# Decoder layer on one core: head halves outside and batches inside, 512-column projections, the last stages of a batch beside the next batch's attention

## The chip, the core and the metric

The kernel runs on one core of a Trainium2 chip. The metric is the device time of one execution in microseconds (us). TensorE (PE) does the matmuls, VectorE (DVE), ScalarE (ACT) and GpSimd (POOL) the rest, and SyncE (SP) issues the transfers. Each engine works through its own list of instructions in order and waits on semaphores for the others.

## The reference

One decoder layer with post-norm on x of 4 batches, 256 tokens and 256 channels, in fp32:

```python
x = _layernorm(x + attn(x))      # 16 heads of 128; q, k with rmsnorm; causal mask and ALiBi bias
x = _layernorm(x + xattn(x, ctx))
x = _layernorm(x + ffn(x))
# attn
q, k = rmsnorm(x @ Wq, q_rms_w), rmsnorm(x @ Wk, k_rms_w)
scores = q @ k.T / sqrt(128) - slope[h] * dist      # causal
y = rmsnorm(softmax(scores) @ (x @ Wv), subln_w)
attn = y @ Wproj                 # 2048 to 256
# xattn: attention = softmax((ctx Wq' + bq)(ctx Wk' + bk)'), result[l, m] = sum_n x[l, n] attention[m, n]
# ffn: 256 to 1024 to 256; weights quantised to -1, 0, 1 times their mean size, inputs to 8 bits by row
h = sigmoid(bitlinear(x, w_gate)) * bitlinear(x, w_up); out = bitlinear(h, w_down)
```

## The kernel before

**Preparation.** The contexts' queries, keys, energies and exponentials are made first, and x is turned into `xT_hi` and `xT_lo`, two parts whose products with `w_hi` and `w_lo` (three for each of two blocks of 128 channels: six matmuls) give the projection.

**Attention.** There are 64 steps. Head by head (outside), batch by batch (inside), a step n projects q, k and v of one head and batch, 384 columns for each of two token tiles (`qkv(0)` and `qkv(1)`, L482), and carries three earlier ones on: of n-1 the normed q and k are turned (L493) and the scores made (L505, L506), of n-2 the probabilities are turned (L499) and multiplied with v (L512 to L514), of n-3 the normed y is turned (L521). VectorE adds a bias with the mask and finds the negative maximum in one operation (L835), norms q and k (L791) and y (L812), copies the turned probabilities (`pT`, L817) and sums squares (L797, L804). ACT takes squares (L635, L673), exponentials and copies. GpSimd raises sums to -1/2 (`qk_rstd` L315, `y_rstd` L310), splits the next head's weights into high and low parts (L276, L280) and halves the bias in place. The steps run in a hardware loop of eight, seven trips, after eight steps written out. The weights of a head are loaded once; three feed-forward pieces are rounded, turned and copied in each trip. Every turned y is kept in `yT` (64 of them).

**Tail.** The output projection (L422, 16 heads for each of eight token tiles, two passes for each fp32 matmul) is done afterwards: four tiles' worth starts while the last heads drain, the others fill TensorE between the last stages. These run tile by tile, `m` in 0 to 8, each half a tile behind the other: residual and layer norm (moments L845, L846; GpSimd's power L355; application on VectorE L851), `x1T`, mixing with the cross attention (L557), norm, quantising (L900 to L904), gate and up (L587), hidden product (L865), its maximum (L886), rounding on ACT (L694), `hq` (L895), `hT` (L564), down (L572, L908), norm and store.

The order of every engine's work is written out by hand; there is no planner.

Of the kernel before, what the change touches and what calls it, by code (L numbers as in the profile page):

```python
# [14 lines left out]
P = 128  # L35
# [3 lines left out]
BANK = 512  # L39


def decoder_kernel(nc, x, ctx_in, wq, wk, wv, wproj, q_rms, k_rms, subln, xwq, xbq, xwk, xbk,
# [10 lines left out]
    STEPS = H * B  # L53
    PAIR = 2 * B
    TRIPS = H // 2
    EARLY = -(-TT * H // 6)
    CROSS_STEP = 3
    FF_STEP = 5
    SPLITS = 3
    VW = D + 1  # L60
    S0, S1 = slice(0, P), slice(P, 3 * P)
    SLOPE0 = 2.0 ** -0.5
    assert D == P and CC == P and T == 2 * P and C == 2 * P and B == 4 and H % 2 == 0
    assert TRIPS == FC and FF_STEP + 3 == PAIR

    ctx = ExitStack()
    with ctx:
# [3 lines left out]
        def sem(name):  # L71
            return ctx.enter_context(nc.semaphore(name))


# [3 lines left out]
        w_raw = sb("w_raw", [P, 2, KC, 3, D])  # L78
        w_hi = sb("w_hi", [P, 2, KC * 3 * D], F32R)
        w_lo = sb("w_lo", [P, 2, KC * 3 * D], F32R)  # L80
        bias = sb("bias", [P, 2, 3 * P])
        wp = sb("wp", [P, H, C])
        yT = sb("yT", [P, STEPS, T])
# [3 lines left out]
        minus_half = sb("minus_half", [P, TT])  # L87
        vecs = sb("vecs", [P, 7])
        bq_col, bk_col, qk_scale, sub_scale = vecs[:, 3:4], vecs[:, 4:5], vecs[:, 5:6], vecs[:, 6:7]
        sq = sb("sq", [P, TT, 2, D + 1])  # L90
        sqy = sb("sqy", [P, TT, VW])
        qk_sum, qk_rstd = sb("qk_sum", [P, TT, 2]), sb("qk_rstd", [P, TT, 2])
        y_sum, y_rstd = sb("y_sum", [P, TT]), sb("y_rstd", [P, TT])
        qk_n = sb("qk_n", [P, TT, 2, D])
        qT = sb("qT", [P, T])
        kT = sb("kT", [P, T])
# [4 lines left out]
        v_sb = sb("v_sb", [P, B, TT, VW])  # L101
        y_n = sb("y_n", [P, TT, D])


        prep = yT[:].rearrange("p n t -> p (n t)")
        ctx_sb = prep[:, 0:NT * CC].rearrange("p (n c) -> p n c", n=NT)
        ctxT = prep[:, 1024:1024 + B * T]
        qcT = prep[:, 2048:2048 + B * T]
        kcT = prep[:, 3072:3072 + B * T]
        xw_sb = prep[:, 4096:4096 + 2 * CC].rearrange("p (a c) -> p a c", a=2)  # L110
        xwT = prep[:, 4352:4352 + 2 * CC].rearrange("p (a c) -> p a c", a=2)
        attn_sum = prep[:, 4608:4608 + NT]
        abs_w = prep[:, 5120:5120 + F]
        attn_raw = prep[:, 11264:11264 + NT * T].rearrange("p (n t) -> p n t", n=NT)
        attn = sb("attn", [P, NT, T])
        neg_xmax = sb("neg_xmax", [P, NT])
# [4 lines left out]
        ff_round = sb("ff_round", [P, C])  # L121
        ff_q = sb("ff_q", [P, C], BF16)
        w_sum = sb("w_sum", [P, 6])
        w_total = sb("w_total", [P, 3])
        w_scale = sb("w_scale", [P, 3])
        w_inv = sb("w_inv", [P, 3])


        res = sb("res", [P, 3, C])
        stats = sb("stats", [P, 3, nc.vector.BN_STATS_DIM])  # L130
        mean_var = sb("mean_var", [P, 3, 2])
        var_eps = sb("var_eps", [P, 3])
        ln_rstd = sb("ln_rstd", [P, 3])
        x1 = sb("x1", [P, C])
        x2 = sb("x2", [P, 2, C])
        fin = sb("fin", [P, 2, C])
        x1T = sb("x1T", [P, KC, P])
        x_most, x_scale, x_inv, h_most, h_scale, h_inv, down_scale = (sb(n, [P, 1]) for n in (
            "x_most", "x_scale", "x_inv", "h_most", "h_scale", "h_inv", "down_scale"))
        gate_up_scale = sb("gate_up_scale", [P, 2])  # L140
        round_col, table = sb("round_col", [P, 1]), sb("table", [P, 1])
        x_round = sb("x_round", [P, C])
        xq = sb("xq", [P, C], BF16)
        xqT = sb("xqT", [P, KC, P], BF16)

        sig, hid, h_round = ff_raw[:, 0, 0:F], ff_raw[:, 0, F:2 * F], ff_raw[:, 1, 0:F]
        hq = sb("hq", [P, F], BF16)
        hT = sb("hT", [P, FC, P], BF16)
# [784 lines left out]
```

## Time and profile before

| what | us |
|---|---|
| median of three runs | 435.4 (434.58 to 435.41) |
| profiled execution, span from the first to the last instruction | 432.9 |
| TensorE busy | 401.9 (93%) |
| VectorE busy | 327.7 (76%) |
| ACT busy | 254.4 (59%) |
| GpSimd busy | 220.2 (51%) |

The page gives each engine's busy time and the chain of work that ended last, followed back from the last instruction. The windows give the same busy times for a stretch, with the clock that TensorE was granted there (1.00 is full) and what the transfers moved. The chain in order of time gives each instruction only the time by which the next link was later, so for TensorE it is issue time, while a matmul's duration in the timeline also has its way through the array and overlaps with the next.

### The profile page before, as it was taken

What the parts mean: (1) busy time and instruction counts of PE and PEld (TensorE: products, weight loads), DVE (VectorE), ACT (ScalarE), POOL (GpSimd) and SP (SyncE); (2) the same over time, 40 slices, a digit from 0 to 9 for tenths busy, and PEclk for the clock granted to TensorE, in tenths of its full rate; (3) what the DMA queues carried; (4) which work ended last, traced back from release to release, by engine and by line L of the source; (5) the groups of instructions that cost most, each with busy time, mean ns of one, the idle gap of its engine ahead of it and who ended that gap; (6) DMA issues with size and microseconds to landing.
All of it is one profiled execution on the core that took longest, in us unless ns stands there. A gap on an engine that the chain in (4) does not pass through costs nothing.

```text
span 432.9 us, 9595 instructions
## 1 busy us (share of the span) xinstructions
PE 401.9 (93%) x2605; PEld 361.1 (83%) x2612; DVE 327.7 (76%) x1000; ACT 254.4 (59%) x750; POOL 220.2 (51%) x368
## 2 busy tenths in 40 slices
PE   4979999999999999999999999999999899999552
PEld 3668899999999999999999999999988677777321
DVE  0777987887797798788779779878822788888862
ACT  3486777677676776767767677676722333333321
POOL 3633667676675776767767677675501122222210
PEclk9999999999999999999999999999999999999965
DMA  8980010110101101011010110000000000000000
GB/s 223 316 251 2 2 36 3 38 37 0 36 0 36 36 0 36 0 36 36 0 36 0 36 36 0 0 0 0 0 2 0 2 0 15 12 14 12 13 14 24
DMA packets 21747, 14.52 MB, mean 34 GB/s; under 512 B 1760, under 2 KB 21472, under 8 KB 21728
## 3 DMA queue, kind: packets, MB, share of 16 engines
q1 hardware_dynamic: 21728, 14.29, 11.2%
q8 instruction: 9, 0.15, 0.2%
q14 instruction: 10, 0.08, 0.1%
HBM read 13.24 MB, written 1.05 MB: 33 GB/s over the span
## 4 chain that ended last, share of the span: by engine, by line
PE 86%; DVE 5%; ACT 4%; issue 2%; DMA 1%; POOL 1%; SPq 0%; POOLq 0%; DVEq 0%
PE ps L482 30%; PE ps L422 11%; PE ps L493 7%; PE ps L506 6%; PE ps L499 5%; PE ps L512 4%; PE ps L505 3%; PE ps L514 3%; PE ps L513 3%; PE ps L521 3%; PE ps L587 3%; PE ps L572 2%; ACT hT L696 2%; DMA x_sb<-in_x 1%; PE ps L557 1%
## 5 line engine op out<-in xcount | busy, mean ns | idle before, releaser
L315 POOL TENSOR_TENSOR qk_rstd<-qk_sum,minus_half 128x2 f32<-128x2 f32 x128 | 88.5, 692 | 92.6 <-DVE qk_sum L797 90.8
L482 PE MATMUL ps<-w_hi,xT_hi 128*128 128x384 f32 x256 | 96.9, 378 | 2.3 <-DVE qk_n L791 1.4
L482 PE MATMUL ps<-w_hi,xT_lo 128*128 128x384 f32 x256 | 86.5, 338 | 0.0
L482 PE MATMUL ps<-w_lo,xT_hi 128*128 128x384 f32 x256 | 86.3, 337 | 0.0
L797 DVE TENSOR_REDUCE qk_sum<-sq 128x2 f32<-128x258 f32 x128 | 53.6, 419 | 30.8 <-ACT sq L635 29.1
L635 ACT ACTIVATE sq<-ps 128x256 f32<-128x256 f32 x128 | 49.1, 384 | 34.6 <-PE ps L482 34.4
L791 DVE TENSOR_TENSOR qk_n<-ps,qk_rstd 128x256 f32<-128x256 f32 x128 | 54.2, 423 | 18.8 <-POOL qk_rstd L315 17.8
L422 PE MATMUL ps<-wp,yT 128*128 128x256 f32 x256 | 62.2, 382 | 0.0
L310 POOL TENSOR_TENSOR y_rstd<-y_sum,minus_half 128x2 f32<-128x2 f32 x64 | 49.0, 766 | 24.6 <-DVE y_sum L804 20.9
L673 ACT ACTIVATE sqy<-ps 128x258 f32<-128x258 f32 x64 | 24.8, 387 | 58.5 <-PE ps L514 58.5
L422 PEld LDWEIGHTS ps<-wp,yT 128*128 128x128 f32 x256 | 46.7, 190 | 5.9
L482 PEld LDWEIGHTS ps<-w_hi,xT_hi 128*128 128x128 f32 x256 | 48.4, 189 | 3.0 <-DVE qk_n L791 1.7
L482 PEld LDWEIGHTS ps<-w_lo,xT_hi 128*128 128x128 f32 x256 | 48.6, 190 | 0.0
L482 PEld LDWEIGHTS ps<-w_hi,xT_lo 128*128 128x128 f32 x256 | 48.0, 188 | 0.0
L352 POOL TENSOR_SCALAR var_eps<-mean_var 128x1 f32<-128x1 f32 x24 | 7.0, 292 | 79.6 <-DVE mean_var L846 79.6
L835 DVE CUSTOM_DVE_ANT_0 score<-ps,bias 128x128 f32<-128x128 f32 (+1 forms) x128 | 40.3, 352 | 2.8 <-PE ps L506 2.8
L493 PE MATMUL ps<-ident,qk_n 128*128 128x128 f32 x256 | 38.7, 273 | 0.8 <-DVE qk_n L791 0.6
L506 PE MATMUL ps<-kT,qT 128*128 128x256 f32 x128 | 38.2, 380 | 0.0
L280 POOL TENSOR_TENSOR w_lo<-w_raw,w_hi 128x256 fp32r<-128x256 f32 x48 | 35.4, 738 | 4.0
L817 DVE COPY pT<-ps 128x384 f32<-128x384 f32 x64 | 35.1, 548 | 2.6 <-PE ps L499 2.5
L493 PEld LDWEIGHTS ps<-ident,qk_n 128*128 128x128 f32 x256 | 31.1, 140 | 5.0 <-issue 3.2
L639 ACT COPY v_sb<-ps 128x128 f32<-128x128 f32 x128 | 34.0, 266 | 0.0
(126 smaller groups left out, 846.9 us busy)
## 6 DMA issues: line engine op xcount, KB each, us to landing
w_raw<-in_L_attn_Wq SPq DMA_DIRECT2D x16, 128.0 KB, 2.2
w_raw<-in_L_attn_Wk SPq DMA_DIRECT2D x16, 128.0 KB, 2.3
w_raw<-in_L_attn_Wv SPq DMA_DIRECT2D x16, 128.0 KB, 2.3
wp<-in_L_attn_Wproj SPq DMA_DIRECT2D x1, 2048.0 KB, 16.1
ff_raw<-in_L_ffn_w_gate SPq DMA_DIRECT2D x1, 1024.0 KB, 8.6
ff_raw<-in_L_ffn_w_up SPq DMA_DIRECT2D x1, 1024.0 KB, 11.0
ff_raw<-in_L_ffn_w_down SPq DMA_DIRECT2D x1, 1024.0 KB, 13.0
out<-fin SPq DMA_DIRECT2D x8, 128.0 KB, 1.7
```

The source lines that it names most:

```text
L280: pool.tensor_tensor(lo, raw, hi, ALU.subtract).then_inc(s_split, 1)
L310: pool.tensor_tensor(y_rstd[:], y_sum[:], minus_half[:], ALU.pow).then_inc(s_ry, 1)
L315: pool.tensor_tensor(qk_rstd[:, t, :], qk_sum[:, t, :], minus_half[:], ALU.pow).then_inc(s_rs[t], 1)
L422: last = pe.matmul(ps[:, u % 2, 0:C], yT[:, h * B + b, t * P:(t + 1) * P], wp[:, h, :], start=(h == 0), stop=(h == H - 1))
L482: last = pe.matmul(ps[:, t, 0:3 * D], xa[:, k, tok], wa[:, r, k * 3 * D:(k + 1) * 3 * D], start=(i == 0), stop=(i == len(parts) - 1))
L493: last = pe.transpose(dst[:, t * P:(t + 1) * P], qk_n[:, t, a, :], ident[:])
L506: pe.matmul(ps_s[:, S1], qT[:, P:T], kT[:], start=True, stop=True).then_inc(s_s, 1)
L635: act.activation(sq[:, t, :, 0:D], ps[:, t, 0:2 * D].rearrange("p (a d) -> p a d", a=2), ACT.Square).then_inc(s_sq[t], 1)
L791: dve.tensor_tensor(qk_n[:, t], ps[:, t, 0:2 * D].rearrange("p (a d) -> p a d", a=2), r, ALU.mult).then_inc(s_qkn[t], 1)
L797: dve.tensor_reduce(qk_sum[:, t, :], sq[:, t], AX.X, ALU.add).then_inc(s_ss[t], 1)
L817: dve.tensor_copy(pT[:], ps_pT).then_inc(s_pT, 1)
L835: last = dve.tensor_tensor_reduce(score[:, s], ps_s[:, s], bias[:, r, s], 1.0, 3e38, ALU.add, ALU.min, neg_max[:, t:t + 1])
```

## The change

Outside are now two halves of the heads, inside the four batches, and innermost the eight heads of a half: eight blocks of eight steps, all written out without a loop. The six pieces of weights of a half (four of two heads' q and k, two of four heads' v) are split once and stay resident, 512 columns each. The query-key projection of a step (three steps ahead, `LAG`) makes one token tile of two heads; every second step has a value projection of four heads and one tile. ACT and VectorE split the first half's pieces with GpSimd; in steps 24 to 30 VectorE makes the high part and GpSimd the low part of the second half's.

The output projection of a step follows three steps later into one bank, summed over the eight heads of a block; the first half's sum is added onto `x_sb` in place. `wp` is multiplied by `sub_scale` beforehand. After the second half's block of a batch its two tiles go through the last stages in steps of their own offsets from `late_start` (the second tile four steps after the first, for the last batch both together), beside the next batch's attention. Layer norms are applied on GpSimd, and so is `x_round`. Sigmoid becomes tanh of half the argument, with the factors folded into scales. The cross attention's preparation moves from the start into slots "a", "b" and "c" of steps 3 to 16, the feed-forward weights' into steps 12 to 24, 1024 columns at a time by two comparisons instead of eight trips of 256.

Banks: A and B take the projections, TB the turned q, k and also the turned y, SP the scores and also the turned probabilities, Y the values' product, O the output projection, F and G the side work. For the last batch's two tiles SP, Y, TB, O and A, B, F, G are used.

The order in a step n, by engine. TensorE: `project_qk(n + 3)`; q and k of n turned; the probabilities of n-1 turned; `project_v` in even steps; slot "a"; output projection of n-3; y of n-2 turned; slot "b"; scores of n; values' product of n-1; slot "c". VectorE: `norm(n + 2)`; `y_sum` of n-2; the first half's `split_low`; late work of the tiles at offset 1 (residual, moments), 2 (`xq`), 3 (hidden half 0), 4 (hidden half 1, maximum, scales), 6 (residual, moments); `y_n` of n-2; `pT` of n-1; `qk_sum` of n+3; `split_high`; slot "a"; `wp` scaled (steps 1 and 30); `sum_ff`; `quantise_ff`; slot "b"; the block's sum added (and, in the second half, moments); score operations of n; `x_most` (offset 1), `hq` (offset 4). ACT: square of y; exponentials of n-1; cross exponentials (steps 9 to 12); tanh half 0; squares of n+3; `split_high` of the first half; `qT`, `kT`; value copy; slot "a"; `h_round` (offset 4); `yT`; slot "b"; tanh half 1.

```diff
+LAG = 3
+PREP = {
+    -4: (("a", "x", 0),), -3: (("a", "x", 1),), 0: (("a", "x", 2),), 1: (("a", "x", 3),),
+    3: (("a", "xw", 0),), 4: (("a", "ctx", 0), ("b", "ctx", 1)),
+    5: (("a", "qc", 0), ("b", "qc", 1)), 6: (("a", "kc", 0), ("b", "kc", 1)),
+    8: (("a", "en", 0),), 9: (("a", "en", 1),), 10: (("a", "en", 2),), 11: (("a", "en", 3),),
+    13: (("a", "at", 0),), 14: (("a", "at", 1),), 15: (("a", "at", 2),), 16: (("a", "at", 3),),
+    17: (("a", "ws", 0),),
+    19: (("a", "ff", 0),), 20: (("a", "ff", 1),), 21: (("a", "ff", 2),), 22: (("a", "ff", 3),),
+    23: (("a", "ff", 4),), 24: (("a", "ff", 5),),
+}
+FIRST_SPLIT = {-4: (0, 1), -3: (2,), -1: (3,), 0: (4,), 1: (5,)}
+SECOND_SPLIT = {24: 6, 25: 7, 26: 8, 28: 9, 29: 10, 30: 11}
+LATE_STEPS = 7
+LATE_SLOTS = ((0, "a", "x1T"), (0, "c", "mix"), (2, "a", "xqT"), (2, "c", "gate0"), (2, "c", "up0"),
+              (3, "b", "gate1"), (3, "b", "up1"), (5, "a", "hT"), (5, "c", "down"))
...
+    def late_start(tile):
+        b, t = tile // TT, tile % TT
+        start = HB * (B + b) + HB + LAG
+        return start if b == B - 1 else start + 4 * t
...
+            sp.dma_start(x_sb[:, 0:TT, :], x_d[:, 0:TT, :]).then_inc(s_x[0], 16)
+            for c in range(3):
+                load_piece(c)
+            sp.dma_start(x_sb[:, TT:NT, :], x_d[:, TT:NT, :]).then_inc(s_x[1], 16)
+            load_wp(0)
+            for c in range(3, 6):
+                load_piece(c)
...
+            for n in steps():
+                if 0 <= n - 2 < N:
+                    pool.wait_ge(s_ssy, n - 1)
+                    wait(pool, s_yn, n - 2)
+                    pool.tensor_tensor(y_rstd[:], y_sum[:], minus_half[:, 0:TT], ALU.pow).then_inc(s_ry, 1)
+                for c in FIRST_SPLIT.get(n, ()):
+                    split_first(c)
+                if n in SECOND_SPLIT:
+                    split_second(SECOND_SPLIT[n], (0, 1))
+                for tile in late(n, 1):
+                    wait(pool, s_mv[2], tile - 2)
+                    layer_norm(1, tile, res2, x2[:, tile % 3])
...
+                    pool.tensor_tensor(qk_rstd[:, t], qk_sum[:, t], minus_half[:], ALU.pow).then_inc(s_rs, 1)
+                if n in SECOND_SPLIT:
+                    split_second(SECOND_SPLIT[n], (2, 3))
...
+                    pe.wait_ge(s_qkT, n + 1)
+                    wait(pe, s_pT, n)
+                    pe.matmul(ps_s[:, S0], qT[:, 0:P], kT[:, 0:P], start=True, stop=True)
+                    pe.matmul(ps_s[:, S1], qT[:, P:T], kT[:], start=True, stop=True).then_inc(s_s, 1)
...
+                for tile in late(n, 4):
+                    t = tile % TT
+                    hidden(tile, 1)
...
+                    link(dve.tensor_reduce(h_most[:, t:t + 1], hid[:, t], AX.X, ALU.max, apply_absolute_value=True))
...
+                    dve.tensor_tensor(y_n[:], ps_y[:, :, 0:D], y_rstd[:].unsqueeze(2).to_broadcast([P, TT, D]),
                                       ALU.mult).then_inc(s_yn, 1)
...
+                    dve.tensor_copy(pT[:], ps_s).then_inc(s_pT, 1)
...
+                if n in SECOND_SPLIT:
+                    split_high(SECOND_SPLIT[n])
...
+                if 18 <= n < 24:
+                    quantise_ff(n - 18)
```

## Rows read from the trace of the kernel before

**Rows 1.** Windows: us of each engine, TensorE's granted clock, transfers' share and GB/s.

```profile
10.00:20.00 10.00, 10.00 (x39) 6.85 (x39) 6.51 (x14) 4.86 (x13) 6.67 (x12) 1.00 1.02 302
100.00:200.00 100.00, 100.00 (x707) 96.27 (x706) 82.31 (x270) 69.73 (x229) 68.73 (x107) 1.00 0.07 20
400.00:420.00 20.00, 12.44 (x65) 6.88 (x64) 14.81 (x40) 7.15 (x11) 4.54 (x10) 0.83 0.04 14
420.00:433.00 13.00, 2.92 (x16) 1.80 (x16) 4.42 (x11) 2.25 (x2) 0.74 (x2) 0.56 0.06 20
```

**Rows 2.** Chain in order of time, 214 to 217 us: start, issue time, what.

```profile
214.48 0.44 PE ps L493 x4
214.92 0.33 PE ps L499 x3
215.25 1.06 PE ps L482 x6
216.31 0.22 PE ps L505 x2
216.53 0.43 PE ps L506 x2
```

**Rows 3.** Timeline of one attention step, TensorE and VectorE: start, duration.

```profile
208.76 0.42 PE L482 MATMUL ps<-w_hi,xT_hi 128*128 128x384 f32 x1
...
211.00 0.42 DVE L812 TENSOR_TENSOR y_n<-ps,y_rstd 128x256 f32<-128x256 f32 x1
...
211.35 0.55 DVE L817 COPY pT<-ps 128x384 f32<-128x384 f32 x1
...
212.73 0.28 DVE L835 CUSTOM_DVE_ANT_0 score<-ps,bias 128x128 f32<-128x128 f32 x1
...
212.94 0.42 DVE L835 CUSTOM_DVE_ANT_0 score<-ps,bias 128x256 f32<-128x256 f32 x1
...
213.18 0.42 PE L482 MATMUL ps<-w_hi,xT_hi 128*128 128x384 f32 x1
```

**Rows 4.** Timeline of TensorE in the tail, 361 to 365 us.

```profile
361.51 1.03 PE L587 MATMUL ps<-wuT,xqT 128*128 128x512 bf16 x4
362.38 1.89 PE L422 MATMUL ps<-wp,yT 128*128 128x256 f32 x8
364.10 0.38 PE L550 MATMUL ps<-ident,x 128*128 128x128 f32 x2
```

**Rows 5.** Groups by line and shape: busy us, mean ns; idle time before.

```profile
L315 POOL TENSOR_TENSOR qk_rstd<-qk_sum,minus_half 128x2 f32<-128x2 f32 x128 | 88.5, 692 | 92.6 <-DVE qk_sum L797 90.8
...
L280 POOL TENSOR_TENSOR w_lo<-w_raw,w_hi 128x256 fp32r<-128x256 f32 x48 | 35.4, 738 | 4.0
...
L865 DVE SCALAR_TENSOR_TENSOR ff_raw<-ps,gate_up_scale,ff_raw 128x512 f32<-128x512 f32 x16 | 11.9, 747 | 3.2 <-PE ps L587 2.9
...
L895 DVE TENSOR_SCALAR hq<-ff_raw 128x1024 bf16<-128x1024 f32 x8 | 5.5, 683 | 1.4 <-ACT ff_raw L694 1.4
...
L720 DVE TENSOR_TENSOR xT_lo<-ps,xT_hi 128x512 fp32r<-128x512 f32 x4 | 2.7, 689 | 12.3 <-ACT xT_hi L596 12.3
```

**Rows 6.** Timeline of VectorE after the last attention step.

```profile
326.67 0.42 DVE L804 TENSOR_REDUCE y_sum<-sqy 128x2 f32<-128x258 f32 x1 [3.12 <-ACT sqy L673]
327.89 0.42 DVE L812 TENSOR_TENSOR y_n<-ps,y_rstd 128x256 f32<-128x256 f32 x1 [0.80 <-POOL y_rstd L310]
```

**Rows 7.** Timeline of VectorE for the last tile.

```profile
404.91 0.39 DVE L876 TENSOR_TENSOR res<-ps,x_sb 128x256 f32<-128x256 f32 x1
...
408.18 1.22 DVE L886 TENSOR_REDUCE h_most<-ff_raw 128x1 f32<-128x1024 f32 x1
...
409.82 0.41 DVE L891 TENSOR_TENSOR res<-ps,x 128x256 f32<-128x256 f32 x1
...
410.73 0.18 DVE L846 BATCH_NORM_AGGREGATE mean_var<-stats 128x2 f32<-128x6 f32 x1
```

**Rows 8.** Timeline: the first scores of the kernel.

```profile
26.01 0.43 PE L505 MATMUL ps<-kT,qT 128*128 128x128 f32 x2
```

More of the change, by code:

```diff
@@ new lines, in project_v @@
+            def project_v(v):
+                four, t = v // TT, v % TT
+                b, which, half = four // 2 % B, four % 2, four // (2 * B)
+                c = piece_of("v", which)
+                if b == 0 and t == 0:
+                    if half == 0:
+                        pe.wait_ge(s_lo_dve, c + 1)
+                        pe.wait_ge(s_lo_pool, 2 * (c + 1))
+                    else:
+                        pe.wait_ge(s_lo_pool, 12 + 4 * (c + 1))
+                if v > 0:
+                    pe.wait_ge(s_nm, 2 * v + 1)
+                tok = slice(b * T + t * P, b * T + (t + 1) * P)
+                parts = [(xa, wa, k) for k in range(KC) for xa, wa in ((xT_hi, w_hi), (xT_hi, w_lo), (xT_lo, w_hi))]
+                for i, (xa, wa, k) in enumerate(parts):
+                    last = pe.matmul(bank["A" if v else "O"], xa[:, k, tok], wa[:, c, k * BANK:(k + 1) * BANK],
+                                     start=(i == 0), stop=(i == len(parts) - 1))
+                last.then_inc(s_v, 1)
@@ L592, in _ @@
+                for item, i in slots[n, "c"]:
+                    spare(item, i)
         @block.scalar
         def _(act):
[L594 to L603 removed]
@@ L671, in step, with half_gate @@
+            def half_gate(tile, f):
+                t = tile % TT
+                wait_filled(act, f"gate{f}", tile)
+                act.wait_ge(s_gus, tile + 1)
+                wait(act, s_hr, tile - 1)
+                act.activation(sig[:, t, f * BANK:(f + 1) * BANK], turn(f"gate{f}", tile), ACT.Tanh,
+                               scale=gate_up_scale[:, t, 0:1]).then_inc(drained(f"gate{f}", tile), 1)
+            for n in steps():
+                if 0 <= n - 2 < N:
                     act.wait_ge(s_y, n - 1)
@@ new lines, in _ @@
+                for tile in late(n, 3):
+                    half_gate(tile, 0)
+                if n == FIRST:
+                    spare("x", 0)
+                j = n + LAG
+                if 0 <= j < N:
+                    t = j % TT
+                    act.wait_ge(s_qk[t], j // 2 + 1)
+                    wait(act, s_ss, j - 1)
+                    act.activation(sq[:, t, :, 0:D], bank["AB"[t]].rearrange("p (a d) -> p a d", a=4),
+                                   ACT.Square).then_inc(s_sq, 1)
@@ new lines, in _ @@
+                for c in FIRST_SPLIT.get(n, ()):
+                    split_high(c)
+                if 0 <= n < N:
+                    act.wait_ge(s_t, n + 1)
+                    act.activation(qT[:], ps_qT, ACT.Copy, scale=q_scale[:, head(n):head(n) + 1])
+                    act.copy(kT[:], ps_kT).then_inc(s_qkT, 1)
+                if n % 2 == 0 and 0 <= n // 2 + 1 < N // 2:
+                    v = n // 2 + 1
+                    act.wait_ge(s_v, v + 1)
+                    wait(act, s_y, 4 * (v // 2 - 1))
+                    act.copy(v_sb[:, v // 2 % 2, v % 2, :, 0:D],
+                             bank["A" if v else "O"].rearrange("p (a d) -> p a d", a=4)).then_inc(s_vc, 1)
@@ L707, in _ @@
+                if 0 <= n - 2 < N:
+                    act.wait_ge(s_ty, n - 1)
+                    act.copy(yT[:], ps_yT).then_inc(s_yT, 1)
+                for item, i in slots[n, "b"]:
+                    spare(item, i)
+                for tile in late(n, 3):
+                    half_gate(tile, 1)
         @block.vector
```

1252 lines of the change are left out of this document (615 added, 637 removed).

## The prediction

> **What bounds the kernel now.** First the page: TensorE is busy for 93% of a 432.9 us span and holds 86% of the chain that ended last. A share of busy time says nothing of stages, so next the windows [rows 1]: between 100 and 200 us TensorE is busy all the time at the full clock, VectorE for 82%; after 400 us TensorE is busy for 12.4 of 20 and then 2.9 of 13 us, and its granted clock falls to 0.83 and 0.56. So there are two regimes: 64 attention steps and the tail beside the leftover output projection, both bound by TensorE, and some 30 us at the end bound by a chain through all engines.
>
> The chain of waits gives TensorE's prices as issue time [rows 2]: a projection of six 384-column matmuls 1.06 us, four transposes 0.44, three 0.33, the scores 0.22+0.43. One step is 4.42 us from one tile-0 projection to the next [rows 3]; what is left of it, 4.42-2x1.06-0.44-0.33-0.65=0.88, is the attention-by-value matmuls (0.66) and two transposes (0.22). TensorE waits for nobody there, because two projections and the loop's other matmuls cover the way of one head through ACT, VectorE and GpSimd.
>
> **The change part by part.** *TensorE's work.* Per step, two 6x384 projections go. One 6x512 query-key projection comes (two heads), and in every even step a 6x512 value projection (four heads). The columns are the same, 4608 a step, the matmuls 9 for 12. No row shows this type at 512 columns. Bound from below: the bf16 matmuls of 512 columns, four in 362.38-361.51=0.87 us, 0.2175 each [rows 4]. From above: in proportion, 1.06/6x4/3=0.235 [rows 2]. I take 0.2175, the row with the same columns, keep 0.235 for the range. The output projection moves into the step: eight passes take 364.10-362.38=1.72 us, 0.215 each [rows 4], and a step has four, 0.86.
>
> A step's TensorE work W is then: 1.31 (projection) +0.44+0.33+0.22 (transposes) +0.86+0.65+0.66 = 4.47 in odd steps, +1.31 (values) = 5.78 in even ones; 5.12 on the mean, 328 in all. One token tile's last stages cost two transposes 0.22, mixing 0.86 (four passes), gate and up 8x0.2175=1.74, and the bf16 transposes and the down projection about 1.4: 4.2 us. The preparation (x, contexts, energies, weights) is about 13 us inside steps 0 to 31.
>
> *The loop of waits.* This is what I think decides. Scores and the turned probabilities now share one bank; the y, q and k transposes share another; VectorE does y_n before the pT copy; late work, splitting and quantising stand in VectorE's and GpSimd's queues between these. So scores(n) to scores(n+1) has a length of its own, R:
> - scores: 0.65 of issue [rows 2] and an estimated 0.2 until the last one has landed: 0.86
> - the two score operations, 212.73 to 212.94+0.42: 0.63 [rows 3]
> - norm of 512 columns: like xT_lo, 0.69 [rows 5]; then y_sum 0.42, and 327.89-327.09=0.80 until y_n can start, which is GpSimd's power and two hand-overs [rows 6]
> - y_n 0.42, pT 0.55, three overlaps of 0.07 as between y_n (211.00+0.42) and pT (211.35) [rows 3], 0.1 to TensorE.
>
> R is 4.3 us; the norm also waits for its rstd (after pT: sum 0.62, power of four columns 0.94, from the two-column 0.69 and an estimated 0.12 a column), which makes it 4.4. That is just under W=4.47: a plain step stays bound by TensorE, and anything put into VectorE's queue in an odd step shows, less the free time it meets (0.34 before the score operations, 0.80 beside GpSimd's power). In even steps 1.4 us more are free.
>
> *Steps 0 to 31.* W: 16x(5.78+4.47)+13=177. Over that: steps 18 to 23 quantise 1024 columns in two operations, 0.68 as hq and 1.28 (0.75+512/0.96 ns, from [rows 5]); R is 4.4+1.96-0.07-0.34=5.95 against W 4.9 in the odd ones: 3x1.05=3. Steps 24, 25, 26, 28, 29 and 30 split the second half's weights: VectorE's copy 0.68 follows qk_sum, GpSimd waits for it, then does two subtractions (2x0.74 [rows 5]), the power 0.94, two more subtractions, and only then the next y power: 0.62+0.68+0.08+1.48+0.94+1.48+0.73+0.05+0.35+0.55=7.0 us a step, 42 for six where W gives 31: 11. Scaling wp (steps 1 and 30), the weights' sums (12 to 17) and first pieces: 3. Sum 194 us.
>
> *Steps 32 to 41*: W, 51.
>
> *Steps 42 to 62.* Each batch's two tiles run four steps apart. In the steps with hidden half 1, maximum and scale, VectorE does 0.75+1.64+0.2 [rows 5, 7] ahead of y_n; less 0.80 R is 6.2, W 5.55. With residual and moments of the third norm (410.91-409.82=1.1 [rows 7]) plus quantised x (0.5), less 0.80, and the maximum of x before (0.8): R=6.0, W 5.46. The steps between are even ones, with 6.64 and 7.08 of W over R. Eight steps: 2x(6.2+7.1+6.0+6.6)=52, where W alone is 49.5. Steps 42 to 49 have one tile fewer: 49; 50 to 57: 52; 58 to 62 lose the projections: 30.
>
> *Start.* Scores(0) stood at 26.0 us [rows 8]. Now only batch 0's x and one piece of weights stand before the first projection, but the rest of x (0.75 MB) and three pieces (1.5 MB) come first at the 302 GB/s of [rows 1], about 11 us, and TensorE waits for that x before the second projection. With the fill of three steps I estimate scores(0) at 21 us: 5 won.
>
> *End.* After scores(63) nothing covers: score operations, exponentials, transposes, values, two norms' worth of hand-overs and the last output projection, 0.86+0.63+0.85+0.55+0.55+0.84+0.43+0.42+0.80+0.42+0.4+0.4+1.0, and some 2.3 of late work in VectorE's way: 10.4 us. The last tile took 28.0 us from its first residual (404.91) to the end [rows 7]; now both tiles of batch 3 go side by side through the single VectorE, ACT and GpSimd, and wait for each other at the norms, maxima and hidden halves: +4.6, an estimate. The clock is low there as it is after 420 us [rows 1]; the 28.0 has that in it.
>
> Sum: 21+194+51+49+52+30+10.4+32.6=440 us of span. The profiled span is 432.9 and the median 435.4, 2.5 more; so 442.5 on the scale of the runs. The estimated terms are as likely rounded up as down; I round to 442.
>
> *Edits at nothing.* The halving of the bias on GpSimd goes, and its mask is now scaled inside the score operation: both engines' time there was free. ACT's work per step stays near 3.3 us under a W of 4.5, so its wider squares, value copies and tanh halves hide under TensorE; its five vector loads come while x is on its way. On SP the fourth piece of weights waits for the first split, and behind it queue the contexts, the feed-forward weights and the other half of wp: the first of them is needed in step 3, some 15 us later; if the split were late by more than that, each us would show. The loop over pairs becomes a straight list; no row prices a branch apart, so I take nothing, between 3 us won (0.4 a trip, an estimate of what I can't place beyond the steps' 4.42) and 3 us lost to fetching a longer program.
>
> As for the matmul's price, the Trainium skill ("TensorE: Matmul & The Clock Gate", Back-to-back issue gap) gives an isolated matmul of N columns N/2.4+2.5 ns, 216 ns at 512. The gates of [rows 4] agree; the 384-column row (0.177 measured, 0.1625 by the rule) doesn't. By the rule the sum stays; by the row it is the 8 us of rival B.
>
> **The rivals.** *A, TensorE stays the bound (faster).* If the loop R is shorter than I count, for instance if queues run ahead so that late work fills gaps, every step takes W: 21+177+51+47+49.5+27.5=373, +10.4+32.6=416, on the scale of the runs 419. For it: the old kernel ran at 100% TensorE with VectorE at 82%, and a step has slack of 1.4 us every second time. Against: the banks are single, so nothing runs ahead. It decides if R with the extra work stays under W in odd steps, that is if the VectorE extras cost under a third of what I count. Chance 0.2; between A and my case, with part of the 24 us of stalls and still faster, 0.07.
>
> *B, 512 columns cost in proportion (slower still).* 9x0.0175=0.16 us a step, in the some 48 steps where W rules: 8 us, 450. For: the 384-column row carries a cost over its columns. Against: the gates don't. Chance 0.18.
>
> *C, the gain of the start is not there and GpSimd is slower.* GpSimd's power ran 0.69 to 0.77 us in the old kernel; it now also does all the norms. 0.1 us more in some 30 R-bound steps is 3 us, and a start like the old one 5: 450. Chance 0.13. The Trainium skill ("GPSIMD Engine Reference", Specifications) says that GpSimd's SBUF interfaces are shared with VectorE and contended by its two-input and 2-port operations; no row here separates that, and it would push the same way.
>
> *D, no change:* stalls of some 16.5 us instead of 24 would give 435 to 436. Chance 0.04.
>
> **How the numbers follow.** My case has 0.38. A measurement tells 0.2% (0.9 us). Faster: 0.20+0.07=0.27; same 0.04; slower 0.38+0.18+0.13=0.69. The range leaves out A's lower half and the joint of B and C: 421 to 457. My case alone would be 434 to 449, by the size of its estimated terms.
>
> **What would show it.** In the profile after: 512-column projections of six matmuls at 1.31 us; scores(0) near 21 us; between 220 and 265 us TensorE at 95% or more; in steps 24 to 30 a step of about 7 us in which VectorE's norm waits for GpSimd; from 265 us on TensorE near 93%, with pT or the scores named as what it waits for, behind the maxima; after the last score some 43 us with TensorE mostly idle. If TensorE shows 99% from 25 to 370 us, A holds. If the projections stand 1.41 us apart, B. If steps 0 to 3 are slow, the start was misjudged. The prediction is wrong above all if VectorE's late work doesn't stop TensorE.

## The result, and the profile after

The changed kernel takes 460.5 us (median of four runs, 459.9 to 462.2), the kernel before 435.0 beside it: a ratio of 1.060, 95% interval 1.057 to 1.063. I had forecast 442 us with a range of 421 to 457. The direction is right, the time lies 3.5 us above the range, and the size of the loss, 25 us, is nearly four times the 6.6 I gave. The profiled execution has a span of 458.1 us; the forecast in that measure was 440, so 18 us are to be found.

First the page of the changed kernel: busy times, and the tenths of TensorE, VectorE and the granted clock in 40 slices.

```profile
PE 408.5 (89%) x2420; PEld 337.5 (74%) x2420; DVE 296.8 (65%) x802; ACT 248.5 (54%) x582; POOL 186.4 (41%) x308
...
PE   1869999999999999898999999999899998976544
...
DVE  1457546677588876566566676587876779576462
...
PEclk9989999999999999999999999999999999999666
```

TensorE works nearly as much as before (408.5 for 401.9 us), VectorE less (296.8 for 327.7). What grew is TensorE's idle time, 49.6 us for 31.0. The windows of the changed kernel, cut at the start, at stages of like steps, at the last scores (408.1) and where the output projection of the last step is done (419.2), say where. The columns are those of [rows 1].

```profile
0.00:28.70 28.70, 15.02 (x52) 11.25 (x53) 10.45 (x17) 11.91 (x21) 14.66 (x46) 0.96 0.89 279
28.70:169.00 140.30, 138.44 (x857) 119.00 (x857) 98.42 (x250) 88.50 (x218) 47.87 (x57) 1.00 0.08 27
169.00:218.80 49.80, 44.67 (x259) 36.80 (x258) 29.66 (x79) 23.96 (x61) 31.65 (x41) 1.00 0.10 33
218.80:271.40 52.60, 52.60 (x322) 45.89 (x321) 32.23 (x92) 29.62 (x75) 17.02 (x20) 1.00 0.00 1
271.40:408.10 136.70, 128.96 (x793) 106.31 (x791) 98.69 (x290) 78.41 (x183) 58.41 (x104) 1.00 0.02 5
408.10:419.20 11.10, 9.46 (x62) 7.38 (x63) 6.66 (x22) 4.65 (x11) 4.96 (x11) 1.00 0.01 1
419.20:458.10 38.90, 19.32 (x84) 10.86 (x82) 20.64 (x54) 11.47 (x15) 11.83 (x30) 0.67 0.04 14
```

And the kernel before, from its first scores [rows 8] to the last tile's first residual [rows 7]:

```profile
26.00:405.00 379.00, 371.75 (x2475) 341.23 (x2482) 301.26 (x944) 233.88 (x708) 203.91 (x325) 1.00 0.06 18
```

The 25.2 us of span come from three places. The start is 28.7 us long instead of 26.0: +2.7. Between the first scores and the last residual stand 390.5 us (419.2-28.7) instead of 379.0: +11.5, of which TensorE's idle time is 9.1 (16.4 for 7.3) and its work 2.4. What follows with nothing beside it takes 38.9 us instead of 27.9: +11.0, at a granted clock of 0.67.

Against my own terms, read at the starts of the scores of steps 0, 32, 42, 50, 58 and 63:

| term | forecast | measured | error |
|---|---|---|---|
| start, to scores(0) | 21 | 28.7 | +7.7 |
| steps 0 to 31 | 194 | 190.1 | -3.9 |
| steps 32 to 41 | 51 | 52.6 | +1.6 |
| steps 42 to 49 | 49 | 51.8 | +2.8 |
| steps 50 to 57 | 52 | 54.0 | +2.0 |
| steps 58 to 62 | 30 | 30.9 | +0.9 |
| scores(63) to the end | 43 | 50.0 | +7.0 |

Three sizes are wrong. **The first is TensorE's price.** A plain step of the changed kernel, TensorE's timeline:

```profile
235.91 0.40 PE L428 MATMUL ps<-w_hi,xT_hi 128*128 128x512 f32 x1
236.15 0.39 PE L428 MATMUL ps<-w_lo,xT_hi 128*128 128x512 f32 x1
236.38 0.39 PE L428 MATMUL ps<-w_hi,xT_lo 128*128 128x512 f32 x1
236.61 0.60 PE L540 MATMUL ps<-ident,qk_n 128*128 128x128 f32 x4
```

The starts are 0.23 us apart, not 0.2175, and nothing is idle between them at a granted clock of 1.00. Steps take 4.57 and 5.96 us in turn, where I had 4.47 and 5.78; their difference, 1.39 us, is one value projection, 0.232 a matmul. That is my rival B (0.235, in proportion to 384 columns [rows 2]). The bf16 gates took 0.2175 [rows 4]: the row with the same columns has another type. The projections' parts are fp32r, as the rows of `w_lo` print it (the matmul rows say f32), and each makes one matmul. That the type decides is my reading of these rows; no run changed the type alone.

**The second is the start.** VectorE and TensorE in the changed kernel:

```profile
9.30 0.15 DVE L803 TENSOR_SCALAR vecs<-vecs 128x1 f32<-128x1 f32 x1 [9.30 <-DMA vecs<-in_L_attn_subln_w]
...
9.70 0.68 DVE L765 TENSOR_TENSOR xT_lo<-ps,xT_hi 128x512 fp32r<-128x512 f32 x1
10.30 1.82 DVE L727 TENSOR_TENSOR w_lo<-w_raw,w_hi 128x512 fp32r<-128x512 f32 x2
...
11.04 0.79 PE L428 MATMUL ps<-w_hi,xT_hi 128*128 128x512 f32 x1 [5.81 <-DVE w_lo L727]
11.63 0.63 PE L428 MATMUL ps<-w_lo,xT_hi 128*128 128x512 f32 x1
...
25.64 0.50 PE L447 MATMUL ps<-w_hi,xT_hi 128*128 128x512 f32 x1 [2.20 <-DVE qk_n L798]
```

VectorE's first instruction waits until 9.30 us for a vector of 128 numbers on its way among the weights, and xT_lo and the low part of the weights stand behind it. I had written that these loads come "while x is on its way". Then the first projections run 0.43 us a matmul, nearly twice the later spacing, though the window from 11 to 16 us shows a granted clock of 1.00; no run says why. Two of the fill's query-key projections and its second value projection wait 0.93, 0.60 and 2.20 us for a norm that frees their bank, which has squares, sum, GpSimd's power (1.0) and the norm itself in a row, and behind the last of these waits the clock falls (0.59 from 25.6 to 29.4 us; the last section has more on it). From the first projection to scores(0) are 17.7 us; I had put the whole fill at 10.

**The third is the end**, which is the next section's main subject.

Two forecasts held. Between 219 and 271 us TensorE is busy all the time. Beside late work the steps with hidden half 1 and its maximum take 6.2 to 6.3 us (6.2 forecast), and TensorE's matmuls wait there for one thing above all, as the waits of 271 to 408 us show (us in total, times, longest):

```profile
PE ps L570 <- DVE y_n L864: 5.9, 7, 1.3
PE ps L545 <- ACT prob L662: 0.7, 1, 0.7
```

The steps with the third norm took 5.6 us, less than my 6.0, with TensorE busy all the time: of my two kinds of stalled steps only one stalls. In turn the even steps take 7.4 and 7.7 us where I had 7.1 and 6.6, since the gate and up matmuls of both halves, 1.74 us, all stand between the scores of two steps, and I had put only 0.86 there. VectorE's timeline in a step with the maximum has y_n behind it:

```profile
299.45 1.22 DVE L841 TENSOR_REDUCE h_most<-ff_raw 128x1 f32<-128x1024 f32 x1
...
301.52 0.42 DVE L864 TENSOR_TENSOR y_n<-ps,y_rstd 128x256 f32<-128x256 f32 x1
```

### The profile page after: what moved, and what is told of

Same layout as the page of the kernel before. It is cut to its first block and busy times, and to the rows that moved or that the text cites. A ratio compares the mean times of both kernels' runs of the same rounds, so it can differ in the third digit from the quotient of the medians.

```text
span 458.1 us, 7853 instructions
## 1 busy us (share of the span) xinstructions
PE 408.5 (89%) x2420; PEld 337.5 (74%) x2420; DVE 296.8 (65%) x802; ACT 248.5 (54%) x582; POOL 186.4 (41%) x308
## 5 line engine op out<-in xcount | busy, mean ns | idle before, releaser
L385 POOL TENSOR_TENSOR qk_rstd<-qk_sum,minus_half 128x4 f32<-128x4 f32 x64 | 67.9, 1061 | 87.8 <-DVE qk_sum L875 87.8
L918 DVE CUSTOM_DVE_ANT_0 score<-ps,dist 128x128 f32<-128x128 f32 (+1 forms) x128 | 40.6, 355 | 57.4 <-PE ps L578 57.3
L428 PE MATMUL ps<-w_hi,xT_hi 128*128 128x512 f32 x128 | 57.7, 451 | 7.3 <-DVE w_lo L727 5.8
L681 ACT ACTIVATE sq<-ps 128x512 f32<-128x512 f32 x64 | 38.1, 596 | 30.0 <-PE ps L428 29.8
L798 DVE TENSOR_TENSOR qk_n<-ps,qk_rstd 128x512 f32<-128x512 f32 x64 | 44.0, 687 | 13.3 <-POOL qk_rstd L385 13.3
L428 PE MATMUL ps<-w_hi,xT_lo 128*128 128x512 f32 x128 | 51.3, 401 | 0.0
L428 PE MATMUL ps<-w_lo,xT_hi 128*128 128x512 f32 x128 | 50.9, 398 | 0.0
L864 DVE TENSOR_TENSOR y_n<-ps,y_rstd 128x256 f32<-128x256 f32 x64 | 26.9, 421 | 35.9 <-POOL y_rstd L369 35.8
L875 DVE TENSOR_REDUCE qk_sum<-sq 128x4 f32<-128x516 f32 x64 | 43.5, 680 | 0.0
L545 PE MATMUL ps<-ident,prob 128*128 128x128 f32 x192 | 32.0, 276 | 1.7 <-ACT prob L662 1.6
```

The costliest lines, as they stand in the source:

```text
L385: pool.tensor_tensor(qk_rstd[:, t], qk_sum[:, t], minus_half[:], ALU.pow).then_inc(s_rs, 1)
L428: last = pe.matmul(bank["AB"[t]], xa[:, k, tok], wa[:, c, k * BANK:(k + 1) * BANK], start=(i == 0), stop=(i == len(parts) - 1))
L545: last = pe.transpose(ps_s[:, i * P:(i + 1) * P], prob[:, i * P:(i + 1) * P], ident[:])
L681: act.activation(sq[:, t, :, 0:D], bank["AB"[t]].rearrange("p (a d) -> p a d", a=4), ACT.Square).then_inc(s_sq, 1)
L798: dve.tensor_tensor(qk_n[:, u % 2, t], bank["AB"[t]].rearrange("p (a d) -> p a d", a=4), qk_rstd[:, t, :].unsqueeze(2).to_broadcast([P, 4, ...
L875: dve.tensor_reduce(qk_sum[:, j % TT], sq[:, j % TT], AX.X, ALU.add).then_inc(s_ss, 1)
```

## The experiments

The start itself varies: with nothing changed there, scores(0) stood at 27.4 to 29.4 us in nine profiled executions. Later stages of unchanged code agree to 0.1 us, but for steps 0 to 23 in two runs (0.3 and 0.5 us more) and for step 31, below. From scores(63) to the end, code that was not changed there took 48.9, 49.6 and 50.0 us, so that a difference of 1 us at the end tells nothing. So I compare stage by stage.

### What the last batch's stages cost: two runs that leave work out

The first leaves out all last stages of tiles 6 and 7, the second also those of tiles 4 and 5 (`range(4)`), with the waits, moments and stores that belong to them; those output rows are not written.

```diff
-        return [tile for tile in range(NT) if n - late_start(tile) == offset]
+        return [tile for tile in range(6) if n - late_start(tile) == offset]
...
```

> Leaves out the last stages of batch 3 (norms, mixing, feed-forward, store of its two tiles). Theory 'uncovered end': everything after batch 3's output projection is exposed, so the span falls from 458.1 to about 421 to 423 (o(63) is complete at 419.2; the tail of tile 5 then ends last), some 36 us. Rival 'stalls in the steps': the end costs what its TensorE work costs, 2 tiles x 4.3 us, and the span falls by 9 to 12 us.

> Leaves out the last stages of batches 2 and 3. Against the run without batch 3's alone this removes the same work once more, but from where it stands beside attention. Theory 'uncovered end': it falls by a further 8.6 us of TensorE work plus about 3 us of stalls, 11 to 14 us, a third of what batch 3's cost. Rival 'stalls in the steps': beside attention the same work costs more than at the end, over 20 us.

Measured: 439.0 us (ratio 1.010, 1.007 to 1.012; span 434.0) and 418.0 us (0.962, 0.960 to 0.964; span 416.0). Leaving out batch 3's stages saves 24.1 us of span (21.5 by the medians), between the two theories, and not the whole uncovered stretch, since tile 5 then shows what it had kept under them. The first run's VectorE after its last y_n:

```profile
418.35 0.68 DVE L910 TENSOR_TENSOR pool_early<-ps,x_sb 128x512 f32<-128x512 f32 x1
419.59 0.69 DVE L790 SCALAR_TENSOR_TENSOR ff_raw<-attn_raw,ps 128x512 f32<-128x512 f32 x1 [0.55 <-ACT attn_raw L650]
420.37 1.22 DVE L841 TENSOR_REDUCE h_most<-ff_raw 128x1 f32<-128x1024 f32 x1
...
428.62 0.48 DVE L854 SCALAR_TENSOR_TENSOR pool_early<-ps,down_scale,pool_early 128x256 f32<-128x256 f32 x1 [4.26 <-PE ps L527]
```

Tile 5's hidden half 1, maximum, turn, down projection and norm all come after the attention. "Last stages beside the next batch's attention" holds in full for four of eight tiles and for most of a fifth. Without tiles 4 and 5 another 18.0 us go. Behind scores(63) it is 16.3: from there to the end it is 26.9 us (434.0-407.15) in the first run and 10.6 (416.0-405.42) in the second. Beside attention, from scores(42) to scores(63), it is 5.0 (136.7 to 131.7); a later start and a slower step 31 in the second run hide 3.4 of these. The theory had 11 to 14 us and its rival over 20 from beside attention: what tiles 4 and 5 cost lies mostly at the end. The 10.6 is what the attention itself leaves there. My 10.4 is near it by luck, as it had 2.3 us of late work in it that this run doesn't have.

### One tile at the end instead of two, and the second a step later

The first run leaves out tile 7's last stages. The second keeps both and changes:

```diff
-        return start if b == B - 1 else start + 4 * t
+        return start + 1 * t if b == B - 1 else start + 4 * t
```

> Leaves out all last stages of tile 7 (the second of batch 3), so that tile 6 goes alone at the end; its output rows are not written. It prices the term of my prediction that two tiles side by side take 4.6 us more than one. Theory 1 (the term is right): the end is 4 to 5 us shorter, about 456 us. Theory 2 (the second tile waits for the first at each GpSimd norm, 1.9 us, and its gate and hidden work runs on the slow clock): 7 to 9 us shorter, 452 us. Theory 3 (side by side is nearly free, the end is the chain of one tile): under 2 us shorter.

> One edit: tile 7 goes through its last stages one step behind tile 6 instead of beside it. Leaving tile 7 out shortened the end by 8.0 us, and each layer norm on GpSimd takes 1.85 us, in which the second tile waits. Theory 1 (what costs is that both tiles want one engine at a time, so half a stage of distance lets them use different ones): 2 to 4 us less, 456 to 459 us. Theory 2 (an engine's list then has each stage of tile 6 ahead of the stage before it of tile 7, so that tile 7 waits a whole stage each time): 3 to 8 us more, 463 to 468 us.

Without tile 7: 453.1 us (1.043, 1.040 to 1.045), span 450.2, scores(63) at 408.2 as in the changed kernel; the end is 42.0 us instead of 50.0. The second tile costs 8.0 us (7.4 by the medians), as theory 2 had it, and not the 4.6 I had estimated. A single tile's end, 42.0 less 11.1 up to the output projection, is 30.9 us where I carried over 28.0 from [rows 7]. These two errors, 3.4 and 2.9, with 0.7 for the stretch before (11.1 for 10.4), are the +7.0. GpSimd of the changed kernel shows one place where tile 7 waits for tile 6:

```profile
422.78 0.19 POOL L360 TENSOR_SCALAR var_eps<-mean_var 128x1 f32<-128x1 f32 x1
423.06 0.55 POOL L361 TENSOR_TENSOR ln_rstd<-var_eps,minus_half 128x1 f32<-128x1 f32 x1
423.70 0.27 POOL L362 TENSOR_SCALAR ln_shift<-mean_var,ln_rstd 128x1 f32<-128x1 f32 x1
424.07 0.55 POOL L363 TENSOR_SCALAR pool_early<-pool_early,ln_rstd,ln_shift 128x256 f32<-128x256 f32 x1
```

A norm now takes GpSimd four instructions and 1.9 us (422.7 to 424.6), three times for each tile; before, it was two, and VectorE applied it. VectorE shows the other place, the two maxima:

```profile
440.97 1.22 DVE L841 TENSOR_REDUCE h_most<-ff_raw 128x1 f32<-128x1024 f32 x1
...
443.04 0.69 DVE L790 SCALAR_TENSOR_TENSOR ff_raw<-attn_raw,ps 128x512 f32<-128x512 f32 x1
443.81 1.22 DVE L841 TENSOR_REDUCE h_most<-ff_raw 128x1 f32<-128x1024 f32 x1
...
445.88 0.69 DVE L931 TENSOR_SCALAR ff_raw<-ff_raw 128x1024 bf16<-128x1024 f32 x1
```

VectorE has no gap from 440.97 on, and tile 6's `hq`, at 445.88, stands behind tile 7's hidden half and maximum, 2.8 us of them. ACT had rounded tile 6's part at 444.2, so that 1.7 us of this is delay.

A step's distance doesn't help: 462.9 us (1.065, 1.061 to 1.069). The start (0.7 later) and a slow stretch (1.6) are in it; from scores(63) to the end it is 51.0 us, 1.0 more, which is no more than the end varies by. The first theory fell, and the second's 3 to 8 us aren't there either.

### TensorE kept busy at the end

Dummy bf16 matmuls stand ahead of TensorE's waits from step 64 on, into a bank of their own (bank B, so tile 7's stages share A, F and G):

```diff
...
+                for _ in range(WARM.get(key, 0)):
+                    pe.matmul(bank["B"], wdT[:, 0, 0:P], wgT[:, 0, 0:BANK], start=True, stop=True)
```

> Adds dummy bf16 matmuls of 512 columns into a bank of their own ahead of TensorE's waits from step 64 on; tile 7's own matmuls use the other banks. Nothing else changes. Theory 1 (the low clock costs time at the end): the granted clock after 410 us goes from 0.83 and 0.67 to above 0.95, the mixing from 3.6 to about 1.8 us, gates and up of both tiles from 6 to under 4, the down projections from 3.6 to 1.8: 4 to 6 us less, about 455 us. Theory 2 (the dummies only stand ahead of real work): no change or up to 3 us more, at a high clock. A clock that stays low would leave it open.

460.7 us (1.058, 1.056 to 1.061): no change, as theory 2 allows. The mixing of both tiles, first in the changed kernel, then here:

```profile
425.16 3.62 PE L506 MATMUL ps<-attn,pool_early 128*128 128x256 f32 x8
```

```profile
427.15 1.89 PE L507 MATMUL ps<-attn,pool_early 128*128 128x256 f32 x8
...
420.00:430.00 10.00, 8.73 (x46) 5.06 (x46) 6.36 (x15) 2.57 (x4) 3.14 (x8) 1.00 0.04 13
430.00:445.00 15.00, 12.46 (x61) 5.48 (x60) 10.64 (x30) 5.64 (x8) 5.65 (x14) 1.00 0.03 10
```

The clock was held at full speed until 445 us, and the mixing took half the time. Yet the end is 50.0 us in both. Counted from scores(63), the dummies put the last output projection off by 1.2 us; the turns of `hq` then began 1.1 us earlier (37.5 for 38.6), and the dummies ahead of the down projection took that back (40.7 and 40.8). The 1.7 us of the mixing and the 1.9 of the gates thus came through only in part. I take it that most of the end is paced by VectorE and GpSimd, whose rows above have nothing to do with TensorE's clock; that is argued and not shown. What the low clock costs with no dummies in the way was not separated.

### The price of a 512-column matmul

```diff
-                    last = pe.matmul(bank["AB"[t]], xa[:, k, tok], wa[:, c, k * BANK:(k + 1) * BANK],
...
+                    for z in range(2):
+                        last = pe.matmul(bank["AB"[t]][:, z * T:(z + 1) * T], xa[:, k, tok],
+                                         wa[:, c, k * BANK + z * T:k * BANK + (z + 1) * T],
...
```

> Each 512-column projection matmul is made as two of 256 columns with the same weights. It prices columns against instructions, where my prediction took 0.2175 us for a 512-column matmul and after shows 0.232 (0.1765 at 384 columns, so about 0.434 ns a column and 10 ns fixed). Theory 1 (that line): a pair takes 2x0.121=0.242 us, and 576 pairs cost 5 to 6 us more where TensorE is the bound, 465 us. Theory 2 (the matmul waits for its weight load, which sets 0.19 us for each): a pair takes 0.35 to 0.38 us, and the time rises by 50 to 80 us.

463.9 us (1.066, 1.063 to 1.070). Pairs of 256 columns are 0.24 us apart:

```profile
238.05 0.40 PE L429 MATMUL ps<-w_hi,xT_hi 128*128 128x256 f32 x2
238.29 0.40 PE L429 MATMUL ps<-w_lo,xT_hi 128*128 128x256 f32 x2
238.53 0.40 PE L429 MATMUL ps<-w_hi,xT_lo 128*128 128x256 f32 x2
238.77 0.60 PE L546 MATMUL ps<-ident,qk_n 128*128 128x128 f32 x4
```

Twice the instructions and twice the weight loads cost 0.04 us for six, 4.61 for 4.57 us a step. Theory 1 held, and theory 2, that the weight load sets the pace, is out. So this matmul costs by the column, 0.45 ns each (0.232/512; 0.46 at 384), and some 7 ns for an instruction. Joining two heads' projections into wide matmuls wins 12x0.1765-9x0.232=0.03 us a step. The Trainium skill ("TensorE: Matmul & The Clock Gate", Back-to-back issue gap) gives N/2.4+2.5 ns for an isolated matmul, 0.216 us at 512 columns; the bf16 gates agree with it, these projections don't, and the measurement decides.

### Late work in the even steps

Tiles 0 to 5 begin their stages one step later, so that the heavy offsets meet the steps with a value projection.

```diff
-        return start if b == B - 1 else start + 4 * t
+        return start if b == B - 1 else start + 4 * t + 1
```

> One edit: the last stages of tiles 0 to 5 begin one step later, so that hidden half 1 with its maximum, the residuals and the moments fall into even steps, where TensorE has a value projection (about 1.4 us more work), instead of odd ones. Theory 1 (the stalls beside attention come from VectorE's late work ahead of y_n in odd steps): the 6.3 us steps at offset 4 (after: 4.8 us of TensorE work) lose their 1.5 us and the even ones stay near 7.4; over the five to six tiles that pass beside attention 5 to 8 us less, about 453 us. Theory 2 (the stalls are a matter of how much work the late steps hold, not of parity): the stall moves into the even steps; 459 to 461 us, the start of the scores of step 63 within 1 us of 408.1.

459.0 us (1.056, 1.053 to 1.058). Beside attention theory 1 holds: from scores(42) to scores(63) 128.1 us instead of 136.7, 8.6 less where it had 5 to 8. TensorE's idle time in that stretch falls from 7.7 to 1.2 us, and its waits for y_n from 5.9 to 0.5. I had named where the free time lies (1.4 us more in even steps), and 8.6 us stood there to be had. But the end takes 57.0 us instead of 50.0, and so the whole missed theory 1's 453. VectorE in this run:

```profile
425.32 0.69 DVE L790 SCALAR_TENSOR_TENSOR ff_raw<-attn_raw,ps 128x512 f32<-128x512 f32 x1
426.11 1.22 DVE L841 TENSOR_REDUCE h_most<-ff_raw 128x1 f32<-128x1024 f32 x1
...
427.94 0.20 DVE L847 TENSOR_SCALAR down_scale<-h_bound,w_scale 128x1 f32<-128x1 f32 x1
428.18 0.42 DVE L924 TENSOR_REDUCE x_most<-pool_early 128x1 f32<-128x256 f32 x1
```

Tile 5's hidden half 1 and maximum, 2.9 us, now stand ahead of the maxima of x of tiles 6 and 7. The output projection of the last step, too, is done 14.8 us after scores(63) instead of 11.1, with TensorE waiting 2.2 us for tile 5's quantised x in front of it. Of 8.6 us won, 7.0 are given back.

### Tiles two steps apart

To keep that gain, tile 5 must start earlier. The second tile of a batch follows two steps behind the first; in the second run, whose edit is shown, all are a step later as well (`+ 1`); the third adds both edits of the next part.

```diff
-        return start if b == B - 1 else start + 4 * t
+        return start if b == B - 1 else start + 2 * t + 1
```

> One edit: the second tile of batches 0 to 2 begins its last stages two steps after the first instead of four, so that tile 5 (the second of batch 2) begins in step 61 and not 63 and less of it is left for the uncovered end. Theory 1 (tile 5's rest stands in VectorE's and GpSimd's queues ahead of tiles 6 and 7): from scores(63) to the end 44 to 47 us instead of 50.0, scores(63) up to 3 us later as the late work is denser in odd steps, 455 to 459 us in all. Theory 2 (the end is the chain of tiles 6 and 7 alone, tile 5's rest lies beside it): the end stays at 49 to 51 us and the time is 460 to 464 us.

> As the run before it, and all six tiles one step later, so that the heavy offsets fall in even steps. The run with the one-step shift alone brought scores(63) 8.8 us forward (399.3 for 408.1) but its end grew from 50.0 to 57.0 us, since tile 5 started in step 64. Here tile 5 starts in step 62. Theory 1 (the end grew because of tile 5): scores(63) at 399 to 402, the end 49 to 52 us, 450 to 454 us in all. Theory 2 (what is won beside attention comes back at the end anyway, because tiles 6 and 7 need the same engines): 457 to 460 us.

> All edits that a run has spoken for: vectors' products later in VectorE's list, the splits behind GpSimd's power of q and k, tiles two steps apart and one step later. Theory 1 (the parts add up): 450 to 454 from the shift and spacing, less 2.6 us at the start and 1 to 2 us in steps 24 to 30: 446 to 450 us, still above 435, since TensorE's own work is what it was and an uncovered end of some 50 us stays. Theory 2 (the parts hide each other, a gain at the start is lost in the slow stretch after step 31): 453 us or more.

473.7 us (1.087, 1.084 to 1.090), 472.3 us (1.084, 1.081 to 1.087) and 468.8 us (1.077, 1.074 to 1.081). All forecasts missed, but for "453 us or more" of the third, whose reason was another. Steps 42 to 57 take 114.4 us in the first instead of 105.8, and single steps 8.8 instead of 7.7. Some 1.7 of these 8.6 us are the clock: step 55 takes 10.1 us where step 47, with the same work, takes 8.4, and the granted clock is 0.70 from 364.5 to 369.5. TensorE's waits from 271 to 425 us have two lines that were not there with four steps between tiles:

```profile
PE ps L570 <- DVE y_n L864: 6.1, 3, 2.0
PE ps L527 <- DVE ff_raw L790: 3.2, 2, 1.6
PE ps L512 <- ACT pool_early L637: 1.7, 3, 0.6
```

L527 is one tile's down projection, L790 the hidden product by which the other gives bank G back; L512 waits for bank F in the same way. The spare work has these two banks only, and at four steps the tiles happen to take turns, as I read it; no run gave it other banks. The end grew as well, to 54.0, 59.6 and 59.4 us, in spite of the earlier tile 5, so that tile 5's start alone doesn't explain the end; why, I have not taken apart. The third run's 3.5 us less than the second's are the splits (2.0) and step 31 (1.6).

### Two orders of the lists

The first run moves the three products of the vectors behind VectorE's first splits, the second puts GpSimd's splits behind its power for q and k (both halves' splits, except in the very first step).

```diff
-            dve.wait_ge(s_vec, 80)
...
+                if n == FIRST + 1:
+                    dve.wait_ge(s_vec, 80)
```

```diff
...
                 if n in SECOND_SPLIT:
-                    split_second(SECOND_SPLIT[n], (2, 3))
+                    split_second(SECOND_SPLIT[n], (0, 1, 2, 3))
```

> VectorE's wait for the five small vectors and its three scalings move from the head of its queue behind its work of the first step. Theory 'the wait for the vectors gates the start': xT_lo starts near 5.9 us instead of 9.7, the first low part near 7.6, the first projection near 9.6 instead of 11.0, scores(0) 1 to 2 us earlier, total 1 to 2.5 us less. Rival 'the weights gate the start' (ACT and GpSimd split them one after the other): the projection still waits for GpSimd's low part, under 0.5 us.

> GpSimd does its subtractions for the weights behind the query-key rstd of the step, in steps -3 to 1 and 24 to 30. Theory 'loop of waits': the steps 24 to 30 fall from 6.0 to 7.3 us to TensorE's 5.0 and 6.4, and the value projection of step 0 no longer waits 2.2 us for the norm; 5 to 8 us less in all. Rival 'TensorE is the bound there anyway': under 2 us less; or the low parts come too late for steps 29 to 35 and it is slower.

The first takes 459.0 us (1.057, 1.055 to 1.060). Its theory held as far as the first projection: `xT_lo` starts at 5.83 us for 9.70, and the first projection at 9.46 for 11.04, waiting for GpSimd's low part now. So the wait for the vectors cost 1.6 us there. Scores(0) stands at 26.05, against 27.4 to 27.7 in the three unchanged starts that had the full clock like it. With the splits later as well (the run with all four edits) the first projection is at 9.21, but scores(0) at 27.55: that order gives the gain back in the fill. The rest of my error at the start is the slow fill.

The second takes 457.4 us (1.053, 1.050 to 1.056), the only edit whose time is lower with an interval clear of the changed kernel's, among kernels that do all the work. Steps 24 to 31 take 47.8 us instead of 49.7, in it and in the run with all four, and TensorE's idle time in steps 24 to 30 falls from 5.1 to 3.3 us. So the power behind two subtractions, which was my reason for stalls there, makes 2 us of them, less than the 5 to 8 us of the theory; what makes the rest is open.

## Why the prediction missed

**What held, and where luck was.** The direction is right, and VectorE's late work ahead of y_n does stop TensorE in odd steps and is free in even ones, as the shift into even steps shows. So rival A fell, which had TensorE never stopped. But the stalls were fewer than I had: from scores(0) to scores(63) I had 352 us of TensorE's work and 24 of stalls; measured are 364.7 busy and 14.7 idle (1.9 in steps 0 to 23, 5.1 in 24 to 31, 7.7 from 42 on). 14.7 is below the 16.5 at which my own sum says "no change", rival D. What kept the result on the slower side were the terms below, which I had too low. The total of this stretch is off by 3.4 us only because 12.7 too little work and 9.3 too many stalls offset one another.

**W, the price of TensorE's step.** The failed choice was "I take 0.2175, the row with the same columns". It measured 0.232, and the halved matmuls show a price by column. It is 0.10 us an odd and 0.18 an even step, 8.8 of the 12.7 us; some 1.4 us in steps 32 to 41 (1.6 measured) and 2.2 of the 4.8 us in steps 42 to 57. In steps 0 to 31 the same excess, 4.5 us, was hidden by stalls that I had set too high, 17 us for 7.0: the quantising steps 18 to 23 take 5.1 us where I had 5.95, and the steps of the splits 5.1 to 7.3, not 7.0 each.

**Start, 21 for 28.7.** "While x is on its way" left out that VectorE's first wait is for all five vectors, 1.6 us at the first projection. More weighs "with the fill of three steps I estimate", 10 us for 17.7: in the fill three projections wait for a norm, and part of it runs at the slow spacing. I had R's length at hand, 4.4 us, and did not use it: seen from behind, four steps of it after the first projection at 11.0 us are 28.6, though no run shows that this is more than a coincidence.

**End, 43 for 50.0.** The mechanism was right (two tiles share VectorE and GpSimd), the sizes not: 8.0 us for the second tile instead of 4.6, and 30.9 instead of 28.0 for one. The 28.0 of [rows 7] has a norm applied by VectorE, no other tile's rest in the lists, and a faster clock in part: the mixing of the last tile took TensorE 1.13 us there and 2.07 in the run without tile 7, its four passes both times. The runs don't separate the three. So my "the 28.0 has that in it", of the low clock, was wrong for this part. That tile 5's rest stretches into the end was in my step numbers (it begins in step 63) and in no term.

**The range.** B and the start of C came true together, 442+8+5=455, and the start and the end were worse besides. I had called the joint of B and C unlikely enough to leave out; they have nothing that excludes one another, and the end's estimate had no bound of its own. The other half of C isn't there: GpSimd's power for y took 0.70 us, against 0.77 in the kernel before.

## What to carry to other kernels

Price a matmul from a row of its own type before one of its own width. A step's length is one number and the uncovered start and end two others: work them out from the chain, engine by engine and with every tile that is still on its way, since a change that overlaps stages moves work there. And when a stall beside covered work is removed, look at what the moved work now stands in front of; here 8.6 us won became 1.6.

## What the hardware showed that I had not expected

Step 31 took 6.02 us in six of the profiled executions and 7.6 in six others (the run with halved matmuls left aside), with the same instructions in it. In front of it TensorE had waited 1.9 us for y_n (1.0 in the two runs with the splits later, both 6.02). The granted clock over the step is 1.00 in the first six and 0.78 in the others. Scores of 256 columns, two of the projections that follow, and the window of the run with the vectors later (7.63 us):

```profile
210.46 0.81 PE L578 MATMUL ps<-kT,qT 128*128 128x256 f32 x2
...
212.78 0.63 PE L428 MATMUL ps<-w_lo,xT_hi 128*128 128x512 f32 x1
213.21 0.63 PE L428 MATMUL ps<-w_hi,xT_lo 128*128 128x512 f32 x1
...
209.50:214.50 5.00, 4.77 (x18) 4.01 (x19) 3.04 (x10) 1.45 (x4) 1.71 (x2) 0.66 0.01 3
```

The matmuls are 0.43 us apart instead of 0.23, at the lower of the clock's two levels, though TensorE is busy for 4.77 of the 5 us; the changed kernel's own profile has 1.00 in the same place.

The same makes the start vary. Behind the wait of 2.2 us in front of the second value projection, the window from 25.6 to 29.4 us in the changed kernel (scores(0) at 28.70) and in the run without batch 3's stages (27.68):

```profile
25.60:29.40 3.80, 3.76 (x13) 3.19 (x14) 1.79 (x2) 1.04 (x2) 1.65 (x2) 0.59 1.08 360
...
25.60:29.40 3.80, 3.67 (x19) 3.10 (x20) 2.12 (x7) 1.07 (x2) 2.28 (x3) 1.00 1.10 370
```

Of the nine unchanged starts the three with 1.00 there have scores(0) at 27.4 to 27.7, the two with 0.65 and 0.66 at 28.0 and 28.4, the four with 0.55 to 0.59 at 28.7 to 29.4. So waits of about 2 us in TensorE's work, as the splits and the fill make them, cost up to some 1.6 us more in some executions and nothing in others; what decides which, no run shows. GpSimd's power took 1.06 us for four columns, 0.70 for two and 0.55 for one, so four columns cost 0.36 more than two, where I had estimated 0.24.
